# Decoder layer on one core: the feed-forward stage takes rows in expert order, in one block with the expert stage

## The reference, cut to what matters

```python
# attention stage (16 heads, causal by multiplication), then
x = _layernorm(x + _L0_attn_ref(...))
# expert stage: each row goes through the one expert that its token id names (E = 4)
expert_ids = jnp.minimum(tid // tokens_per_expert, E - 1)
for e in range(E):
    g = silu(hidden @ ctx[e].T); u = hidden @ ctx[e].T
    y = (g * u) @ ctx[e]...
    out = jnp.where((expert_ids == e)[..., None], y, out)
x = _layernorm(x + out)
# feed-forward stage
h = silu(x @ w_gate) * (x @ w_up)            # 512 -> 2048
h_sparse = _sparsify_2to4(h)                 # the 2 largest of each 4 neighbours are kept
x = _layernorm(x + h_sparse @ w_down)        # 2048 -> 512
```

## Time and profile before

| quantity | value |
|---|---|
| median of 3 runs | 1214.02 us (1212.42 to 1217.34) |
| the profiled execution's own time | 1213.86 us |
| its span (first to last instruction) | 1212.1 us, so 1.8 us lie around it |
| PE busy | 1091.1 us, 90% of the span |
| DVE, ACT, POOL busy | 777.5, 485.0, 155.7 us |
| mean granted PE clock | 0.964 of full speed |

### The profile page before, as it was taken

One profiled execution on the slowest core, in us unless ns is written; L12 is line 12 of the kernel. 1 busy time (PEld: TensorE's weight loads), 2 busy tenths in 40 slices (PEclk: granted clock), 3 DMA queues, 4 the chain that ended last, 5 costly groups with the idle time before them and its releaser, 6 DMA issues. The chain is left out here.

```text
span 1212.1 us, 23143 instructions
## 1 busy us (share of the span) xinstructions
PE 1091.1 (90%) x7942; PEld 883.1 (73%) x7943; DVE 777.5 (64%) x1877; ACT 485.0 (40%) x1125; POOL 155.7 (13%) x231
## 2 busy tenths in 40 slices
PE   2898969996999898589994999999999999999995
PEld 2576757775777677468883888888888888888883
DVE  4687768866886888646664284555565545655667
ACT  3387628862885488322222332322122222321220
POOL 1022222222221223301113200000000000000112
PEclk9999989998999899789997999999999999999998
DMA  4787714662475166112234210111001100200001
GB/s 183 186 287 201 181 72 124 175 159 71 126 190 141 53 166 202 43 62 78 80 111 164 71 36 1 35 35 35 1 18 52 35 0 0 69 1 1 35 35 69
DMA packets 56045, 108.65 MB, mean 90 GB/s; under 512 B 5632, under 2 KB 5632, under 8 KB 55936
## 3 DMA queue, kind: packets, MB, share of 16 engines
q1 hardware_dynamic: 53376, 98.86, 27.7%
q0 software_dynamic: 2560, 8.39, 2.0%
HBM read 72.10 MB, written 35.13 MB: 88 GB/s over the span
## 5 line engine op out<-in xcount | busy, mean ns | idle before, releaser
L1420 DVE TENSOR_TENSOR h<-f_bank,fsg 128x512 f32<-128x512 f32 x64 | 44.2, 691 | 191.7 <-PE f_bank L42 180.1
L465 ACT ACTIVATE probs<-bank,nmax 128x384 f32<-128x384 f32 (+3 forms) x256 | 135.6, 530 | 63.7 <-DVE nmax L577 57.8
L354 PE MATMUL bank<-ident,probs 128*128 128x128 f32 x640 | 125.5, 296 | 39.5 <-ACT probs L465 28.5
L1349 ACT ACTIVATE fsg<-f_bank 128x512 f32<-128x512 f32 x64 | 38.3, 598 | 305.8 <-PE f_bank L42 298.5
L567 DVE CUSTOM_DVE_ANT_0 bank<-bank,mask 128x384 f32<-128x384 f32 (+3 forms) x256 | 126.9, 496 | 50.2 <-PE bank L344 41.6
L586 DVE TENSOR_TENSOR pt_lo<-bank,pt_hi 128x384 f16<-128x384 f32 (+3 forms) x256 | 124.7, 487 | 7.3 <-ACT pt_hi L474 6.4
L474 ACT ACTIVATE pt_hi<-bank 128x384 f16<-128x384 f32 (+3 forms) x256 | 112.5, 440 | 27.3 <-PE bank L354 22.7
L370 PEld LDWEIGHTS bank<-v,pt_hi 128*128 128x128 f16 x1920 | 85.0, 97 | 51.9 <-DVE pt_lo L586 24.9
L42 PE MATMUL bank<-x_hi,w_qk 128*128 128x512 f32 x256 | 96.6, 418 | 23.2 <-DVE x_lo L591 22.5
L370 PE MATMUL bank<-v,pt_hi 128*128 128x32 bf16 x1920 | 109.5, 178 | 1.2 <-DVE pt_lo L586 1.2
L727 POOL TENSOR_SCALAR ln_var<-ln_mv 128x1 f32<-128x1 f32 x51 | 13.3, 260 | 750.3 <-DVE ln_mv L716 750.3
(11 more groups left out here) (171 smaller groups left out, 2363.4 us busy)
## 6 DMA issues: line engine op xcount, KB each, us to landing
big_lo<-q_hi_dram SPq DMA_DIRECT2D x32, 256.0 KB, 4.0
big_lo<-q_lo_dram SPq DMA_DIRECT2D x32, 256.0 KB, 4.8
big_lo<-k_hi_dram SPq DMA_DIRECT2D x32, 256.0 KB, 3.9
big_lo<-k_lo_dram SPq DMA_DIRECT2D x32, 256.0 KB, 5.4
sorted_dram<-zero SPq DMA_DIRECT2D x1, 4864.0 KB, 18.2
rows<-sorted_dram SPq DMA_DIRECT2D x19, 256.0 KB, 2.6
expert_dram<-y SPq DMA_DIRECT2D x19, 256.0 KB, 2.0
x_raw<-x_t SPq DMA_DIRECT2D x4, 1024.0 KB, 10.8
```

Source lines behind the costliest of these rows:

```text
L354: ins = pe.transpose(TP[u % TR][:, j * P:(j + 1) * P], probs[u % RP][:, j * P:(j + 1) * P], ident[:, :])
L465: act.activation(probs[u % RP][:, 0:cols(r)], S[u % SR][:, 0:cols(r)], ACT.Exp, bias=nmax[:, r, c:c + 1], accum_out=rsum[:, r, c:c + 1]).t ...
L1349: act.activation(sg[v % 2][:, :], GB[v % 2][:, :], ACT.Silu).then_inc(s_sg, 1)
L1420: dve.tensor_tensor(h[r % 2][:, j, :], UB[v % 2][:, :], sg[v % 2][:, :], ALU.mult).then_inc(s_h, 1)
```

## The change

The expert block and the feed-forward block become one block, `late`. The rows stay in expert order to the end.

- `Route.places`, 23 more small DVE instructions, runs during the last sequence's attention (one at every second unit). It computes for each slot of the padded order the row's place in the expert order without padding (`slot_idx`; padding slots get places beyond row 2047), and for each token its place (`place_idx`).
- After an expert tile's norm POOL scatters it by an indirect DMA to `ordered_dram` (`place`); SP's store is gone.
- SP loads four blocks of 512 rows with plain DMAs (`block_in`) as soon as the tiles that can reach into them have landed. The 16 gathers are gone.
- The first weights are cut one each in tiles 11 to 14, and four after the last tile. In tiles 15 to 18 (`n >= TURN`) one `turn` each is put between PE's own steps, with its two halves on ACT and DVE. These first 512 rows go to `hs`, because `xt`'s place is still taken by the experts' matrices; two SBUF to SBUF DMAs move them later.
- `inner(0, 0)` stands ahead of the last tile's second product (`last(18)`), which follows it.
- POOL inverts the order through a small DRAM array (16 scatters of token numbers, one load), and writes the results itself by indirect DMA (`write`), each write of tile t-4 behind `rstd` of tile t. SP's 16 plain writes are gone.

The diff, cut to its core (`experts` is removed whole; its steps stand unchanged in `late` with other names for some semaphores and banks):

```diff
             def batch(b, more):
+                places = route.places(dve) if not more else None
                 for u in range(-AHEAD_MAX, UPB - AHEAD_LO):
+                    if not more and u > 0 and u % 2 == 0:
+                        next(places, None)
...
+    def places(self, dve):
...
+        for e in range(1, E):
+            did(ready().tensor_tensor(first[:, e:e + 1], first[:, e - 1:e], per[:, e - 1:e], ALU.add))
+            yield
+        did(ready().tensor_tensor(gap[:, :], base[:, :], first[:, :], ALU.subtract))
+        yield
...
+        did(ready().tensor_tensor(at2[:, :, :], at[:, :, :], self.onehot[:, :, :], ALU.mult))
+        yield
+        did(ready().tensor_reduce(self.pos[:, :], at2[:, :, :].rearrange("p e t -> p t e"), AX.X, ALU.add))
+        yield
+        did(ready().tensor_copy(self.place_idx[:, :], self.pos[:, :]))
...
+def late(nc, big, x2, context, ident, tile_expert, slot_idx, place_idx, sorted_rows, ordered_rows, order_dram, weights,
+         gate, up, down, out_rows, N, E, D, I):
+    EARLY = NS - 8
+    TURN = NS - RW
...
+        def landed(n):
+            return [(s_yd[0], (n // 2 + 1) * 16), (s_yd[1], (n + 1) // 2 * 16)]
...
         @block.sync
         def _(sp):
+            def block_in(r):
+                for s, value in landed(r * RW + RW - 1 + E - 1):
+                    sp.wait_ge(s, value)
+                sp.dma_start(x2[:, r * RW:(r + 1) * RW, :], blocks[r]).then_inc(s_in[r], 16)
+            def step(n, q, where):
+                if later(n, 0) and (not isinstance(n, int) or n + 3 < NS):
+                    load(n + 3, (q + 3) % 4)
+                if isinstance(n, int):
+                    if n == EARLY:
+                        for i in range(RING):
+                            weights.load(sp, i, i, (gate, up)[i % 2][0, i // 2])
+                        block_in(0)
+                    if n == EARLY + 3:
+                        block_in(1)
+                    if n == NS - 3:
+                        for i in range(RING, 2 * RING):
+                            weights.load(sp, i, i, (gate, up)[i % 2][0, i // 2])
...
+            tiles(sp, step)
+            block_in(2)
+            sp.wait_ge(s_xTl, RW)
+            sp.wait_ge(s_ey, NS)
+            for i in range(2):
+                sp.dma_start(xt[i][:, :, 0:TW].bitcast(F32), hs[i][:, :, :].bitcast(F32)).then_inc(s_moved, 16)
+            block_in(3)
             chunks(sp, body)
-            for t in range(N // P):
-                sp.wait_ge(s_x3, t + 1)
-                sp.dma_start(out_rows[t], x2[:, t, :]).then_inc(s_out, 16)
-            sp.wait_ge(s_out, N // P * 16)
         @block.gpsimd
         def _(pool):
-            for t in range(N // P):
-                gather(t)
-            ln.start(pool)
-            for t in range(N // P):
-                ln.rstd(pool, t, t % 4)
+            def place(n):
+                wait_apart(pool, s_passed, [(s_ye, n + 1)])
+                pool.indirect_dma_start(ordered_rows, bass.IndirectOffsetOnAxis(slot_idx[:, n:n + 1], 0),
+                                        y[n % 2][:, :], None).then_inc(s_yd[n % 2], 16)
+            def write(t):
+                wait_apart(pool, s_passed, [(s_x3, t + 1)])
+                pool.indirect_dma_start(out_rows, bass.IndirectOffsetOnAxis(order[:, t:t + 1], 0),
+                                        x2[:, t, :], None).then_inc(s_out, 16)
...
+            for n in range(NS):
+                ln2.rstd(pool, n, n % 4)
+                place(n)
...
+            for t in range(NT + RW):
+                if t < NT:
+                    ln3.rstd(pool, t, t % 4)
+                if t >= RW:
+                    write(t - RW)
+            pool.wait_ge(s_out, NT * 16)
         @block.tensor
         def _(pe):
+            def step(n, q, where):
...
+                times_expert(e, EU[i], [ext[h][i] for h in range(2)]).then_inc(s_eu, 1)
+                if where < 2:
+                    x_transposes(n + 1, (q + 1) % 4)
+                if isinstance(n, int) and n >= TURN:
+                    turn(n - TURN)
+                if where > 0:
+                    last(e_last, n - 1, 1 - i)
+                gu_transposes(n, i)
...
-            def body(c, first, last):
+            def body(c, first, ends):
                 for v in range(NR * J):
                     inner(c, v)
                     if first:
+                        if v == 0:
+                            last(expert_of(NS - 1), NS - 1, (NS - 1) % 2)
                         if v in turned_at:
                             turn(turned_at[v])
                             turn(turned_at[v] + 1)
```

536 lines of the change are left out of this document (292 added, 244 removed).

## The result

| kernel | median | runs | ratio to the kernel before, 95% interval |
|---|---|---|---|
| before | 1214.35 us | 20, 1211.19 to 1217.34 | |
| changed | 1218.22 us | 20, 1212.60 to 1224.24 | 1.0038, 1.0023 to 1.0053 |

The change made the kernel slightly slower: by 0.38%, less than the 0.5% that I called the limit of this measurement, but with an interval that excludes no change. The forecast was 1205.5 us (1200 to 1216): the time lies outside that range, and the kernel got slower where I had it faster. The profiled execution took 1221.96 us with a span of 1220.2 us, 8.1 us more than that of before and 3.7 us more than its own median. I account for the 8.1 us of the two profiles first; what is known of the 3.9 us between the medians stands at the end of the part on why the prediction was wrong.

What follows compares the result with a forecast made beforehand. TensorE was taken to bound the expert and feed-forward stages, with waits at their seam and DVE and POOL alternating at the end. 1213.86 - 21.4 (seam) + 1.0 (attention) + 12.0 (end) = 1205.5 us, range 1200 to 1216.

Steps and rivals of the forecast that it cites:

- The seam, -21.4 us: Between experts and feed-forward: all 21.4 us of TensorE's waiting and lowered clock would go; lower bound 0.
- my first sign: Seam: no TensorE idle over 0.3 us from tile 14 to the end of chunk 0, granted clock 1.00 throughout.
- What else moves costs nothing that I can find: First chunk: the 16 scatters of token numbers and small load run on POOL far from its `rstd` pairs, cost nothing.
- Rival B: Seam closes only in part: a late load or half makes TensorE wait, half the gain lost; 1216.2 us, chance 0.10.
- The end, +12.0 us: Last chunk: POOL's writes between `rstd` pairs delay DVE's norms and the last landing; +12.0 us, bounds 5 and 24.
- Rival A: End: DVE locks POOL out during descriptor writing, every write costs 2.22 us; 1217.9 us, chance 0.10.
- Rival C: End: writes don't delay the norms, so about 5 us instead of 12; 1198.5 us, chance 0.08.
- Rival D: Last sequence's attention: DVE pays all 23 added instructions, 4.6 us instead of 1.0; 1209.1 us, chance 0.10.
- The halves in tiles 15 to 18, `block_in` in time, POOL's `place` in the experts: Expert tiles: extra ACT and DVE passes fit, new inputs land in time, the scatter replacing SP's store is hidden.
- the start of the experts: Last sequence's attention: 23 added DVE instructions, mostly covered, cost +1.0 us, bounds 0 and 4.6.

Runs made afterwards that it cites:

- e1: Changed kernel with POOL's 16 scatters of token numbers, and the load behind them, in chunk 1 instead of chunk 0; 1215.7 us.
- e5: e1 with the first four weight cuts one tile later (tiles 12 to 15), loads still issued in tile 11; median moved by 0.9 us.
- e8: Changed kernel with five edits: token-number scatters in chunk 1, later weight cuts, writes 4 to 7 before `rstd(8)`, output wait on SP, place arithmetic moved; 1203.66 us.
- e10: e1 with the 23 small place operations in VectorE's idle time behind the last softmax steps; median 2.7 us under e1.
- e12: e8 with writes 8 and 9 put into POOL's idle stretch ahead of `rstd(12)`; median 1.5 us lower than e8, 0.96% under the kernel before.
- e2: Changed kernel with chunk 0's down weights loaded ahead of the moved halves and last block; last expert `gu` to `rstd(8)` 8.9 us above e1.
- e3: Changed kernel with the output written by SP's plain DMAs in expert order, leaving out the return to token order; 1210.5 us.
- e4: Changed kernel with POOL's writes 4 to 7 ahead of `rstd(8)`; `rstd(8)` to the end fell by 4.4 us, median rose by 2.1 us.
- e7: e1 with 16 scatters of 512 bytes per row into a scratch tensor added in chunk 0; 9.5 us lost between last expert `gu` and `rstd(8)`.
- e13: Changed kernel with down weights loaded first as in e2, token-number scatters begun after the last block landed; first feed-forward product to `rstd(8)` 532.36 or 532.37 us.
- e14: Changed kernel with token-number scatters begun after the last block landed, load order unchanged; first feed-forward product to `rstd(8)` 532.36 or 532.37 us.
- e9: Changed kernel with the 16 token-number scatters in chunk 0 paced, one for each product of `h`; last expert `gu` to `rstd(8)` 535.11 us.

## Why the prediction was wrong

My terms gave 8.4 us less than before, the profile shows 8.1 us more. The 16.5 us between them are 6.3 of the seam, 6.0 of a hole in chunk 0 that stood in no term, 3.6 of the end and 0.6 ahead of the experts.

- **The seam, -21.4 us: right in mechanism, too large.** TensorE is busy from 640 to 680 us at clock 1.00, as my first sign asked of that part. But I took the whole 21.4 us and allowed nothing for less than full speed around it. From the first expert product to `rstd(8)` it was 677.45 us before and is 662.32 in e1, where chunk 0 has no hole: 15.1 us gained. Of the missing 6.3 us, 1.6 is tile 11 (e5), and 2.05 lie ahead of the second `gu`: 1.57 of them between the first two `gu` (7.45 us against 5.88), at a lower granted clock (0.61 against 0.73 over 515 to 530 us). It is not in the code: e8 and e10 have 5.91 us there (0.75 in e10), e12 with the same code 7.46 (0.67). Some 0.7 us are tiles of 6.48 and not 6.41 us, for which I have no cause, and 2 us I can't place.
- **"What else moves costs nothing that I can find": the step that failed.** I asked whether POOL was free for the 16 scatters. It was. What I did not ask is what their transfers meet: SP's 1 MB block and four weight loads in the same microseconds. It cost 5.9 us in the profile of the changed kernel, as a wait for late weights, and 8.8 to 10.4 us in e2, e3, e4 and e7, with engines standing still. I also never listed the down loads, which the kernel before issued at 654.01, ahead of everything, and which now stand behind the moved halves and `block_in(3)`. e1, e13 and e14 show that the scatters cost nothing once they don't meet these loads; how they stop ACT and TensorE stays open.
- **Rival B (the seam closes only in part, by a late load) came nearest**, with a chance of 0.10. It named tiles 15 to 18 and `inner(0, 2)`; the late load was that of the down weights at v = 3, and one of the gate weights in tile 11. That its 1216.2 us lie near the 1218.2 measured is luck: it halves the seam and keeps the end at 12.0 us.
- **The end, +12.0 us: right up to the last landing, then short by a term.** From `rstd(8)` to the last landing it is 26.9 us against 15.6: +11.3. The cycle of 2.5 us and the 4.4 us of block 3 stand as forecast. To this come 4.3 us because POOL's drain has lost its cover. My sum ended at the landing, since in the kernel before the span ended 0.4 us after it; I did not look at what else closes a block on an engine that now works to the last moment.
- **Rival A (a write costs 2.22 us beside DVE) is out** as the price of every write: of the eight writes among the last `rstd` pairs four took 1.34 us, each beside 0.39 us of a norm, and four 1.08. Its mechanism is there in other places: the scatter of token numbers at 681.11 us ran beside 2.2 us of the `beats` comparisons and took 2.20 us, like the one of the earlier trace rows. **Rival C (the writes don't delay the norms) is out** by e4. **Rival D (all 4.6 us of the attention)** is out: 1.4 us, 1.0 forecast.
- **The halves in tiles 15 to 18, `block_in` in time, POOL's `place` in the experts: right.** The wait in front of `place` is 1.46 us in each tile and hidden.
- **The range** left out the upper halves of A and B and with them the case that came, though two of my terms at nothing had no lower bound beside them.

In the sum of the two profiles: -15.1 for seam and experts together (-21.4), +1.6 for the start of the experts (+1.0), +6.0 for the hole (0; 5.9 of it in stretch 3), +15.6 for the end (+12.0). The hole was 5.9 to 10.4 us in five profiles of kernels that have it. The changed kernel's runs scatter over 11.6 us, those of before over 6.2. A hole that changes from run to run and the moving attention stage would explain that, and with it the 3.9 us between the medians; but only one run of the changed kernel was profiled, so this is argued and not shown.

## What to carry to other kernels

A step that moves to an idle engine still has transfers, and they must be placed like work: list for each moved DMA, and for each that it passes, what else the DMA engines carry at that time. Look too at what closes the block: an engine that was done early may have a last duty (here a drain) that nobody saw. And when a kernel is cut at a few marks that every version has, terms of 1 us can be read that medians with 2 us of noise hide, or even show with the wrong sign, as in e4.

## What the runs showed of the hardware

- **Small scatters beside loads.** Beside 16 scatters of 128 pieces of 4 bytes SP's loads of 256 KB or 1 MB took 15 to 20 us to land in the changed kernel and in e9, and 12.4 to 13.3 us in e13 and e14 (3 to 6 us in e1). Single packets of 2 KB took up to 7.3 us in the changed kernel and 8.1 in e14; the median is 0.08. With pieces of 512 bytes (e7) the loads took 9.2 us together, against 8.0 in e1. The Trainium skill ("DMA: Bandwidth & Descriptors", Queues, rings and completion order) says that each DMA engine takes turns between its queues, packet by packet. By that rule small packets would cost the others little; nothing in that rule explains packets of 7.3 us.
- **Engines that stand still.** In e2, e3, e4 and e7 ACT stood for 7.2 to 10.8 us at once and TensorE for up to 1.4 us at a time, with no release that the trace names. A fetch of 16 KB on the instruction queue took 4.4 to 5.0 us in the changed kernel, e3 and e4, against a median of 1.1. Late instructions would explain the standing still, but in e2 and e7 the recorded fetch took 1.0 us, and in e9 one took 4.3 us with nothing lost. So this stays a guess.
- **POOL's drain** at the end of a block took 4.31 us in the changed kernel, 5.62 in e7, which has 16 more scatters in the block, 3.86 with SP's stores (e3) and 2.22 before. What sets its length is open.
- **A write's own cost.** The write at 1212.80 holds POOL for 0.96 us and lands at 1215.51. The Trainium skill ("Perfetto Trace Analysis", DMA Instruction — SWDGE (GPSIMD)) says that its end in the profile is the end of descriptor writing and not of the transfer; the trace agrees.
